# The output projection as two row tiles of TensorE, one step per slice, with a new step order

## The chip, the cores and the metric

The kernel runs on one core of a Trainium2 chip. The metric is the device time of one execution in microseconds (us). Three runs of the kernel before took 1009.82, 1009.85 and 1011.08 us; the median is 1009.85 us. The core has five engines that work in parallel, each in its own written order, and wait for each other by semaphores: TensorE (PE in the rows, its weight loads PEld), VectorE (DVE), ScalarE (ACT), GpSimd (POOL) and SyncE (SP), which issues the DMAs.

## The reference

The input is x (4 x 1024 x 512). A block of windowed attention on 16-channel tokens is followed by a feed-forward block; both are wrapped in layer norms and residual sums. Cut to what matters here:

```python
# tokens of C = 16 channels; q, k, v in two branches of 8 channels, windows of 8 tokens
att = jnp.concatenate([x1, x2], axis=-1) @ proj_w + proj_b      # proj_w is 16 x 16
mu = att.mean(-1, keepdims=True)
var = ((att - mu) ** 2).mean(-1, keepdims=True)
normed = (att - mu) * lax.rsqrt(var + EPS) * ln_w + ln_b
tok = tok + normed
# then: x = x + LN(attn(LN(x)));  x = x + LN(ffn(LN(x)))
# ffn: gate = silu(x @ w_gate * s_gate); up = x @ w_up * s_up; (gate * up) @ w_down * s_down
```

## The kernel before, in words

The 4096 rows are worked on in 8 tiles of 512 rows. The attention of a tile falls into two slices, `p` and `a` of one tile, `b` and `c` of the next. While TensorE computes the feed-forward block of tile t, the other engines and TensorE's gaps compute the attention of tile t+1 and half of t+2. So a tile of the loop holds one feed-forward block and two slices of attention.

A slice runs through steps: `xt` (transposes of x, L581), `qkv` (L589), the products of q and k on VectorE (`qk`, L1093) whose halves GpSimd adds (L924) and VectorE sums (`qk_sum`, L1102), `softmax`, `exp`, the products with v (`pv`, `pv_sum`, the same lines and L933), `attn_out`, then `cat`, `proj`, `square`, `cent_var`, `cent_std`, `cent_out`. `cat` transposes the attention rows of a slice (L600), four of a window's eight rows at a time, and ScalarE copies them into `catt` (L777). `proj` multiplies `catt` by `wproj` (L610). `wproj` is a 128 x 128 matrix that holds the 16 x 16 weights eight times along its diagonal, one block per token of a window, and zeros elsewhere. VectorE adds the bias and writes `cent` (L1159), ScalarE squares it into `csq` (L783), which lies in the memory of `catt`.

`xt`, `qkv`, `cat`, `proj`, `fx` (the transposes of the feed-forward input, L619) and `ln1_fin` (a small matmul for the first norm, L566) share two work banks of PSUM, `ps_w0` and `ps_w1`. A step takes one of them and waits until the step that had it last was read out (`released`, `bank_of`, `bank_free`). In the kernel before `proj` is two steps per slice: `proj 0` (rows 0 to 3 of the windows, bank 0) and `proj 1` (bank 1).

The feed-forward block of a tile runs in 16 groups m. On TensorE a group is `gate` (L629), `up` (L629) and `down` of group m-3 (L649); ScalarE applies silu to gate (L828), VectorE multiplies (`fuse`, L1228), ScalarE and GpSimd split the result in two halves of float16 (`fuse_hi` L834, `fuse_lo` L987). `up` of group m+1 waits for `fuse` of group m, since there is one bank for `up`. 

The order is written out by hand, in tables: `BEFORE` for the part ahead of the first feed-forward block, `STEADY` for tiles 0 to 5 and for the last, `ENDING` for tile 6. In `STEADY` and `ENDING` each step has a slot 3m + i: it stands behind `gate` (i = 0), `up` (i = 1) or `down` and `fuse` (i = 2) of group m, on every engine that takes part in it. SyncE's order comes from the same tables. In the part ahead of the first block ScalarE also casts the 12 parts of the int8 weights to float16 (`cast`, L819); `att_store` of tile 0 (L507: store the attention's rows, then load them as `o1`, L515) waits for all 12 casts, and the load of `xr` (L494) stands behind it in SyncE's queue.

Of the kernel before, what the change touches and what calls it, by code (L numbers as in the profile page):

```python
# [47 lines left out]
Bank = namedtuple("Bank", "ps last")  # L48


def sandwich_kernel(nc, x, qkv_w, conv_w0, conv_b0, conv_w1, conv_b1, proj_w, proj_b, ln_w, ln_b,
                    w_gate, w_up, w_down, s_gate, s_up, s_down, scratch, out):
    with ExitStack() as ctx:
# [245 lines left out]
        START = [("blocks", 0), ("ln1_apply", 0, 0), ("ln1_stats", 0), ("ln1_fin", 0), ("scale_sums", 0),  # L299
                 ("xt", p, 0, 0), ("ln1_apply", 0, 1), ("scale_row", 0), ("token_bias", p), ("xt", p, 0, 1),  # L300
                 ("qkv", p, 0, 0), ("qkv", p, 0, 1), ("scale_pow2", 0), ("qkv", p, 0, 2), ("qkv", p, 0, 3),
                 ("scale_spread", 0), ("qx", p, 0), ("scales", 0)]

        BEFORE = [("qk", p, 0), ("xt", p, 1, 0), ("qk", p, 1), ("xt", p, 1, 1), ("qkv", p, 1, 0), ("qkv", p, 1, 1),
                  ("qk_sum", p, 0), ("qkv", p, 1, 2), ("qk", p, 2), ("qk_sum", p, 1), ("softmax", p, 0),
                  ("qkv", p, 1, 3), ("qx", p, 1), ("qk", p, 3), ("qk_sum", p, 2), ("cast", 0, 0), ("pv", p, 0),
                  ("cast", 0, 1), ("xt", a, 0, 0), ("cast", 0, 2), ("exp", p, 0), ("qkv", a, 0, 0), ("qk_sum", p, 3),
                  ("xt", a, 0, 1), ("token_bias", a), ("pv", p, 1), ("softmax", p, 1), ("pv_sum", p, 0), ("pv", p, 2),
                  ("qkv", a, 0, 1), ("pv_sum", p, 1), ("pv", p, 3), ("xt", a, 1, 0), ("qkv", a, 0, 2), ("warm", 0, 4),
                  ("qkv", a, 0, 3), ("xt", a, 1, 1), ("qk", a, 0), ("pv_sum", p, 2), ("qk", a, 1), ("recip", p),  # L310
                  ("exp", p, 1), ("cast", 0, 3), ("pv_sum", p, 3), ("cast", 0, 4), ("qk_sum", a, 0), ("qkv", a, 1, 0),
                  ("qk", a, 2), ("ln1_stats", 1), ("qx", a, 0), ("qkv", a, 1, 1), ("qk_sum", a, 1), ("qkv", a, 1, 2),
                  ("qkv", a, 1, 3), ("qx", a, 1), ("exp", a, 0), ("ln1_fin", 1), ("attn_out", p), ("ln1_apply", 1, 0),
                  ("softmax", a, 0), ("qk", a, 3), ("cat", p, 0), ("pv", a, 0), ("qk_sum", a, 2), ("qk_sum", a, 3),
                  ("xt", b, 0, 0), ("softmax", a, 1), ("ln1_apply", 1, 1), ("cat", p, 1), ("pv_sum", a, 0),
                  ("proj", p, 0), ("exp", a, 1), ("square", p, 0), ("qkv", b, 0, 0), ("xt", b, 0, 1),
                  ("qkv", b, 0, 1), ("load_xb", 1), ("cast", 0, 5), ("pv", a, 1), ("qkv", b, 0, 2), ("qkv", b, 0, 3),
                  ("pv", a, 2), ("qx", b, 0), ("xt", b, 1, 0), ("pv_sum", a, 1), ("pv", a, 3), ("proj", p, 1),
                  ("pv_sum", a, 2), ("square", p, 1), ("att_store", 0), ("qk", b, 0), ("xt", b, 1, 1), ("cast", 0, 6),
                  ("qkv", b, 1, 0), ("qkv", b, 1, 1), ("pv_sum", a, 3), ("xt", c, 0, 0), ("cast", 0, 7),  # L320
                  ("qkv", b, 1, 2), ("recip", a), ("cent_var", p), ("attn_out", a), ("cent_std", p), ("qkv", b, 1, 3),
                  ("cat", a, 0), ("qx", b, 1), ("cast", 0, 8), ("cent_out", p), ("qk", b, 1), ("qk", b, 2),
                  ("qk_sum", b, 0), ("cat", a, 1), ("proj", a, 0), ("proj", a, 1), ("qk", b, 3), ("qk_sum", b, 1),
                  ("cent_var", a), ("square", a, 0), ("xt", c, 0, 1), ("square", a, 1), ("cast", 0, 9),
                  ("softmax", b, 0), ("qkv", c, 0, 0), ("cent_out", a), ("qkv", c, 0, 1), ("pv", b, 0),
                  ("load_xb", 0), ("token_bias", b), ("qkv", c, 0, 2), ("qk_sum", b, 2), ("qk_sum", b, 3),
                  ("cent_std", a), ("pv", b, 1), ("xt", c, 1, 0), ("warm_cat", a), ("softmax", b, 1), ("exp", b, 0),
                  ("cast", 0, 10), ("pv_sum", b, 0), ("cast", 0, 11), ("qkv", c, 0, 3), ("load_xr", 0),
                  ("qkv", c, 1, 0), ("token_bias", c), ("pv", b, 2), ("pv", b, 3), ("qkv", c, 1, 1), ("pv_sum", b, 1),
                  ("ffn_norm1", 0), ("exp", b, 1), ("xt", c, 1, 1), ("pv_sum", b, 2), ("pv_sum", b, 3),  # L330
                  ("norm1_add", 0), ("qx", c, 0), ("recip", b), ("qkv", c, 1, 2), ("ffn_norm2", 0), ("attn_out", b),
                  ("qkv", c, 1, 3), ("norm2_apply", 0), ("qk", c, 0), ("warm_fx", 0), ("qk", c, 1), ("fx", 0, 0, 0),
                  ("load_xb", 2), ("fx", 0, 0, 1), ("ln1_stats", 2), ("cat", b, 0), ("qk_sum", c, 0)]
# [1046 lines left out]
```

## Time and profile before

| what | value |
|---|---|
| median of three runs | 1009.85 us |
| the profiled execution, its own time | 1010.97 us |
| its span, first to last instruction | 1009.2 us |
| TensorE busy | 906.0 us (90%) |
| VectorE busy | 877.1 us (87%) |
| GpSimd busy | 694.1 us (69%) |
| ScalarE busy | 609.0 us (60%) |
| mean granted clock of TensorE | 0.954 |

The durations of single instructions overlap their successors a little (a product of 2.28 us is followed by the next start 2.20 us later), so sums are best made from start to start. Matmuls of float32 leave two records each, one weight load and one matmul for each of two passes; transposes leave one. The first gate matmul stands at 164.8 us, and the tiles of the loop follow each other every 110.1 us.

### The profile page before, as it was taken

What the parts mean: (1) busy time and instruction counts of PE and PEld (TensorE: products, weight loads), DVE (VectorE), ACT (ScalarE), POOL (GpSimd) and SP (SyncE); (2) the same over time, 40 slices, a digit from 0 to 9 for tenths busy, and PEclk for the clock granted to TensorE, in tenths of its full rate; (3) what the DMA queues carried; (4) which work ended last, traced back from release to release, by engine and by line L of the source; (5) the groups of instructions that cost most, each with busy time, mean ns of one, the idle gap of its engine ahead of it and who ended that gap; (6) DMA issues with size and microseconds to landing.
All of it is one profiled execution on the core that took longest, in us unless ns stands there. A gap on an engine that the chain in (4) does not pass through costs nothing.

```text
span 1009.2 us, 18380 instructions
## 1 busy us (share of the span) xinstructions
PE 906.0 (90%) x6471; PEld 702.4 (70%) x6471; DVE 877.1 (87%) x1309; ACT 609.0 (60%) x1028; POOL 694.1 (69%) x523
## 2 busy tenths in 40 slices
PE   3725627999999999999999999999999999999996
PEld 2514516777777777777777777787778777777773
DVE  4899999999999999999999999999999999553132
ACT  2636634966576855876495657686487665543431
POOL 3556555888679866987778876986788787633323
PEclk9767767999999999999999999999999999999998
DMA  6010070005100510015000510042001300320001
GB/s 178 2 42 0 1 156 11 2 22 128 41 2 1 147 43 21 0 63 124 21 0 5 146 47 10 0 131 56 23 1 60 88 22 1 103 45 22 21 2 42
DMA packets 78318, 46.12 MB, mean 46 GB/s; under 512 B 39608, under 2 KB 72376, under 8 KB 78264
## 3 DMA queue, kind: packets, MB, share of 16 engines
q1 hardware_dynamic: 73400, 45.10, 17.0%
q10 hardware_dynamic: 4864, 0.32, 0.3%
q8 instruction: 32, 0.52, 0.2%
q14 instruction: 22, 0.18, 0.1%
HBM read 28.63 MB, written 16.78 MB: 45 GB/s over the span
## 4 chain that ended last, share of the span: by engine, by line
PE 41%; DVE 22%; POOL 13%; issue 13%; ACT 7%; DMA 2%; POOLq 0%; SPq 0%; DVEq 0%; ACTq 0%
PE ps_gate L629 11%; PE ps_acc L649 11%; PE ps_up L629 11%; DVE prod L1093 7%; POOL sum L933 4%; PE ps_w L589 4%; DVE fuse L1228 2%; POOL cent L458 2%; DVE ps_x L1102 2%; POOL flo L987 2%; DVE attn L1102 1%; PE ps_w L610 1%; DMA xr<-in_L_attn_x 1%; PE ps_w L581 1%; POOL frs L889 1%
## 5 line engine op out<-in xcount | busy, mean ns | idle before, releaser
L1093 DVE TENSOR_TENSOR prod<-ps_x,qkvl 128x2048 f32<-128x2048 f32 x128 | 290.9, 2280 | 2.4 <-POOL sum L933 1.4
L629 PE MATMUL ps_gate<-xhi,wg 128*128 128x256 f16 x1024 | 230.5, 273 | 0.4 <-DVE xlo L1219 0.4
L629 PE MATMUL ps_up<-xhi,wu 128*128 128x256 f16 x1024 | 230.5, 273 | 0.0
L629 PE MATMUL ps_up<-xlo,wu 128*128 128x256 f16 x1024 | 230.5, 273 | 0.0
L629 PE MATMUL ps_gate<-xlo,wg 128*128 128x256 f16 x1024 | 230.5, 273 | 0.0
L987 POOL TENSOR_TENSOR flo<-fuse,fhi 128x512 f16<-128x512 f32 x128 | 148.5, 1161 | 89.1 <-ACT fhi L834 88.3
L828 ACT ACTIVATE gact<-ps_gate,sgate 128x256 f32<-128x256 f32 x256 | 107.2, 470 | 159.4 <-PE ps_gate L629 158.6
L933 POOL TENSOR_TENSOR sum<-prod 128x1024 f32<-128x1024 f32 x64 | 151.4, 2365 | 30.3 <-DVE prod L1093 15.0
L924 POOL TENSOR_TENSOR sum<-prod 128x1024 f32<-128x1024 f32 x64 | 151.1, 2364 | 29.9 <-DVE prod L1093 20.1
L1228 DVE SCALAR_TENSOR_TENSOR fuse<-ps_up,sup,gact 128x256 f32<-128x256 f32 x256 | 110.1, 471 | 69.8 <-PE ps_up L629 61.8
L589 PE MATMUL ps_w<-wqkvl,xt 128*128 128x256 f32 x512 | 137.4, 408 | 21.9 <-ACT xt L747 13.3
L649 PE MATMUL ps_acc<-wd,flo 128*128 128x512 f16 x512 | 153.3, 379 | 0.0
L649 PE MATMUL ps_acc<-wd,fhi 128*128 128x512 f16 x512 | 153.3, 379 | 0.0
L589 PEld LDWEIGHTS ps_w<-wqkvl,xt 128*128 128x128 f32 x512 | 97.3, 204 | 43.3 <-ACT xt L747 18.0
L629 PEld LDWEIGHTS ps_gate<-xlo,wg 128*128 128x128 f16 x1024 | 100.2, 98 | 21.2
L629 PEld LDWEIGHTS ps_gate<-xhi,wg 128*128 128x128 f16 x1024 | 100.7, 98 | 19.8 <-DVE xlo L1219 0.9
L629 PEld LDWEIGHTS ps_up<-xlo,wu 128*128 128x128 f16 x1024 | 100.2, 98 | 13.5
L629 PEld LDWEIGHTS ps_up<-xhi,wu 128*128 128x128 f16 x1024 | 100.2, 98 | 11.4
L756 ACT ACTIVATE qkvl<-ps_w 128x512 f32<-128x512 f32 x128 | 75.4, 598 | 42.4 <-PE ps_w L589 42.2
L649 PEld LDWEIGHTS ps_acc<-wd,flo 128*128 128x128 f16 x512 | 50.1, 98 | 60.4
L834 ACT ACTIVATE fhi<-fuse 128x512 f16<-128x512 f32 x128 | 80.4, 628 | 1.3 <-DVE fuse L1228 1.3
L1102 DVE TENSOR_REDUCE ps_x<-sum 128x256 f32<-128x1024 f32 x64 | 77.6, 1216 | 0.3 <-POOL sum L924 0.3
(148 smaller groups left out, 1383.6 us busy)
## 6 DMA issues: line engine op xcount, KB each, us to landing
xb<-in_L_attn_x SPq DMA_DIRECT2D x64, 128.0 KB, 2.7
attn_rows<-ratt SPq DMA_DIRECT2D x16, 512.0 KB, 3.5
o<-attn_rows SPq DMA_DIRECT2D x32, 256.0 KB, 4.2
xr<-in_L_attn_x SPq DMA_DIRECT2D x16, 512.0 KB
out_x<-y SPq DMA_DIRECT2D x15, 512.0 KB
x<-in_L_ffn_w_gate SPq DMA_DIRECT2D x1, 1024.0 KB, 5.5
xr<-in_L_ffn_w_up SPq DMA_DIRECT2D x1, 1024.0 KB, 8.2
out_x<-y SPq DMA_DIRECT2D x2, 256.0 KB
```

Source lines behind the costliest of these rows:

```text
L589: mm = nc.tensor.matmul(bank.ps[:, 4 * WC * i:4 * WC * i + 4 * WC], xt[:, 2 * wp + i, :], wqkvl[:, br].rearrange("p f x -> p (f x)"), star ...
L629: mm = nc.tensor.matmul(ps[:, HALF * i:HALF * i + HALF], w[:, k, P * j:P * j + P], xs[:, k, rows], start=(k == 0 and part == 0), stop=(k = ...
L649: return nc.tensor.matmul(ps_acc[q][:], f[:, m % SPLITS, HALF * i + P * q:HALF * i + P * q + P], wd[:, 2 * c + i, :], start=(c == 0 and pa ...
L756: nc.scalar.activation(qkvl[:, g, br, :, 2 * wp:2 * wp + 2].rearrange("p f w x -> p w f x"), bank.ps[:].rearrange("p (w f x) -> p w f x", ...
L828: a = nc.scalar.activation(gact[:, m % 2, part], ps_gate[:, part], ACT.Silu, scale=sgate[:, j:j + 1])
L834: nc.scalar.activation(fhi[:, m % SPLITS, :], fuse[:, m % 2, :], ACT.Copy).then_inc(fhi_done, 1)
L924: nc.gpsimd.tensor_tensor(dst.rearrange("p (s c) -> p s c", c=4), s[:, :, 0:4], s[:, :, 4:8], ALU.add).then_inc(half_done, 1)
L933: nc.gpsimd.tensor_tensor(dst.rearrange("p (s j) -> p s j", j=4), s[:, :, 0:4], s[:, :, 4:8], ALU.add).then_inc(half_done, 1)
L987: nc.gpsimd.tensor_tensor(flo[:, m % SPLITS, :], fuse[:, m % 2, :], fhi[:, m % SPLITS, :], ALU.subtract).then_inc(flo_done, 1)
L1093: nc.vector.tensor_tensor(prod[:, half].rearrange("p (s j k) -> p s j k", j=WIN, k=WIN), left[:, :, None, :].broadcast_to([P, 4 * WIN, WIN ...
L1102: nc.vector.tensor_reduce(dst, sum4[:, u % 2, :].rearrange("p (s c) -> p s c", c=4), AX.X, ALU.add).then_inc(sum_done, 1)
L1228: a = nc.vector.scalar_tensor_tensor(fuse[:, m % 2, part], ps_up[:, part], sup[:, j:j + 1], gact[:, m % 2, part], ALU.mult, ALU.mult)
```

## The change: one projection step per slice, on two row tiles

`proj` becomes one step per slice that holds both work banks. Rows 0 to 63 of `catt` (tokens 0 to 3 of each window) are multiplied by the upper left 64 x 64 block of `wproj`, rows 64 to 127 (tokens 4 to 7) by the lower right one. The first result goes to bank 0, the second to bank 1, in turn: 16 matmuls of 64 rows and 64 columns in place of 8 matmuls of 128 rows and 128 columns. VectorE's two additions and ScalarE's two squares stay two, with four tokens of all eight rows each in place of all tokens of four rows. The core of the diff:

```diff
-Bank = namedtuple("Bank", "ps last")
+Bank = namedtuple("Bank", "ps both last")
...
-        def bank_of(step):
-
-            return {"ln1_fin": 0, "fx": step[-1], "xt": step[-1], "qkv": step[-1] % 2, "cat": step[-1],
-                    "proj": step[-1]}[step[0]]
+        def banks_of(step):
+
+            if step[0] == "proj":
+                return 0, 1
+            return (0 if step[0] == "ln1_fin" else step[-1] % 2,)
...
-                        k = bank_of(step)
-                        bank = Bank(ps_w[k], last_use[k])
-                        last_use[k] = (step, tile)
+                        banks = banks_of(step)
+                        bank = Bank(ps_w[banks[0]], ps_w, [(*last_use[k], k) for k in banks if last_use[k]])
+                        for k in banks:
+                            last_use[k] = (step, tile)
...
-            def proj(at, u, bank):
+            def proj(at, bank):
...
-                pe.wait_ge(cat_read, 2 * (2 * at[0] + at[1]) + u + 1)
+                pe.wait_ge(cat_read, 2 * (2 * at[0] + at[1]) + 2)
                 bank_free(bank)
-                for i in range(4):
-                    mm = nc.tensor.matmul(bank.ps[:, P * i:P * i + P], catt[:, u, i, :], wproj[:], start=True, stop=True)
+                for h in range(WIN):
+                    for i in range(2):
+
+                        rows = slice(WC * i, WC * i + WC)
+                        mm = nc.tensor.matmul(bank.both[i][:, WC * h:WC * h + WC], catt[rows, h // 4, h % 4, :],
+                                              wproj[rows, rows], start=True, stop=True)
                 mm.then_inc(proj_done, 1)
...
-                nc.scalar.activation(csq[:, part].rearrange("p h t c -> p (h t c)"),
-                                     cent[:, part].rearrange("p h t c -> p (h t c)"), ACT.Square).then_inc(sq_done, 1)
+                nc.scalar.activation(csq[:, :, part].rearrange("p h t c -> p h (t c)"),
+                                     cent[:, :, part].rearrange("p h t c -> p h (t c)"), ACT.Square).then_inc(sq_done, 1)
...
-                nc.vector.tensor_tensor(cent[:, 4 * u:4 * u + 4].rearrange("p h t c -> p (h t) c"),
-                                        bank.ps[:].rearrange("p (s c) -> p s c", c=C),
-                                        bproj[:, None, :].broadcast_to([P, 4 * WIN, C]), ALU.add).then_inc(proj_read, 1)
+                for i in range(2):
+                    nc.vector.tensor_tensor(cent[:, :, 4 * i:4 * i + 4, :].rearrange("p h t c -> p h (t c)"),
+                                            bank.both[i][:].rearrange("p (s c) -> p s c", c=C),
+                                            bproj[:, None, :].broadcast_to([P, 4 * WIN, C]),
+                                            ALU.add).then_inc(proj_read, 1)
...
-        STEADY = [(0, ("cat", p, 1)), (0, ("proj", p, 0)), (0, ("square", p, 0)), (2, ("qx", a, 1)),
+        STEADY = [(0, ("qk_sum", a, 0)), (0, ("square", p, 0)), (0, ("square", p, 1)), (0, ("proj", p)),
```

All four tables (`START`, `BEFORE`, `STEADY`, `ENDING`) are new. TensorE first, at slice `a` in the middle of a tile. Before (cat, then `proj 0` behind one gate, `proj 1` behind up and down; L600 is cat, L610 proj, L649 down):

```order
L649 MATMUL ps_acc1<-wd,flo 128x512
L600 MATMUL ps_w0<-ident,qkvl 128x128 x4
L600 MATMUL ps_w1<-ident,qkvl 128x128 x4
L629 MATMUL ps_gate<-xhi,wg 128x256
...
L610 MATMUL ps_w0<-wproj,catt 128x128 x4
L629 MATMUL ps_up<-xhi,wu 128x256
...
L649 MATMUL ps_acc1<-wd,flo 128x512
L610 MATMUL ps_w1<-wproj,catt 128x128 x4
L629 MATMUL ps_gate<-xhi,wg 128x256
```

The same place in the changed kernel (L602 is cat, L615 proj, L635 gate and up, L655 down):

```order
L602 MATMUL ps_w0<-ident,qkvl 128x128 x4
L635 MATMUL ps_up<-xhi,wu 128x256
...
L602 MATMUL ps_w1<-ident,qkvl 128x128 x4
L655 MATMUL ps_acc0<-wd,fhi 128x512
...
L655 MATMUL ps_acc1<-wd,flo 128x512
L615 MATMUL ps_w0<-wproj,catt 128x64
L615 MATMUL ps_w1<-wproj,catt 128x64
L615 MATMUL ps_w0<-wproj,catt 128x64
...
L635 MATMUL ps_gate<-xhi,wg 128x256
```

The two cat steps move apart, and 16 small matmuls that change bank at each step follow each other without another instruction between them.

VectorE at the seam between two tiles, that is from `fuse` of group 15 (the first row) to `fuse` of group 0 (the last). Before:

```order
L1228 SCALAR_TENSOR_TENSOR fuse<-ps_up,sup,gact 128x256 x2
L1093 TENSOR_TENSOR prod<-ps_x,qkvl 128x2048
L1102 TENSOR_REDUCE ps_x<-sum 128x256
L1060 BN_STATS bst<-xb 128x6 x8
...
L1054 SCALAR_TENSOR_TENSOR mv<-bst 128x8
L424 UNCONDITIONAL_BRANCH
...
L1159 TENSOR_TENSOR cent<-ps_w,bproj 128x512
...
L1228 SCALAR_TENSOR_TENSOR fuse<-ps_up,sup,gact 128x256 x2
```

In the changed kernel:

```order
L1236 SCALAR_TENSOR_TENSOR fuse<-ps_up,sup,gact 128x256 x2
L1099 TENSOR_TENSOR prod<-ps_x,qkvl 128x2048
L426 UNCONDITIONAL_BRANCH
...
L1108 TENSOR_REDUCE ps_x<-sum 128x256
...
L1166 TENSOR_TENSOR cent<-ps_w,bproj 128x8x64 x2
...
L1236 SCALAR_TENSOR_TENSOR fuse<-ps_up,sup,gact 128x256 x2
L1064 ISA
L1066 BN_STATS bst<-xb 128x6 x8
```

The statistics of the first norm (`BN_STATS`) move from the end of a tile behind the next tile's first `fuse`, the sum (`TENSOR_REDUCE`) across the branch of the loop, and both additions of `proj` now stand together ahead of `fuse` 0.

ScalarE ahead of the first feed-forward block, around the last casts of weights (`wd<-o`, L819 before, L825 in the changed kernel) and the root for the slice `a` of tile 0 (`crs<-cvar`, L808 and L814). Before:

```order
L819 ACTIVATE wd<-o 128x2048
L756 ACTIVATE qkvl<-ps_w 128x2x4x64 x3
L808 ACTIVATE crs<-cvar,epsc 128x64
L747 ACTIVATE xt<-ps_w 128x512
L771 ACT_TABLE_LOAD
L771 ACTIVATE ps_x<-ps_x 128x512
L819 ACTIVATE wd<-o 128x2048 x2
```

In the changed kernel:

```order
L825 ACTIVATE wd<-o 128x2048
L762 ACTIVATE qkvl<-ps_w 128x2x4x64
L753 ACTIVATE xt<-ps_w 128x512
L789 ACTIVATE catt<-cent 128x8x64
L825 ACTIVATE wd<-o 128x2048
L814 ACTIVATE crs<-cvar,epsc 128x64
```

The last two casts now stand ahead of the root, where before they stood behind it.

## Rows read from the trace of the kernel before

**Rows 1.** The page: span and busy time of the engines.
```profile
span 1009.2 us, 18380 instructions
PE 906.0 (90%) x6471; PEld 702.4 (70%) x6471; DVE 877.1 (87%) x1309; ACT 609.0 (60%) x1028; POOL 694.1 (69%) x523
```
**Rows 2.** Busy time by stretch (stretch: length, engines, granted clock, DMA share).
```profile
386.90:497.00 110.10, 108.90 (x804) 84.93 (x803) 107.44 (x157) 74.66 (x129) 87.19 (x63) 1.00 0.18 48
820.00:908.00 88.00, 86.90 (x676) 66.59 (x675) 65.07 (x109) 48.48 (x85) 56.89 (x47) 1.00 0.19 49
```
**Rows 3.** Timeline of DVE in one tile (start, us, line, tile): its idle times.
```profile
521.77 0.88 DVE L1228 SCALAR_TENSOR_TENSOR fuse<-ps_up,sup,gact 128x256 f32<-128x256 f32 x2 [0.37 <-POOL flo L987]
566.78 2.29 DVE L1093 TENSOR_TENSOR prod<-ps_x,qkvl 128x2048 f32<-128x2048 f32 x1 [0.26 <-POOL sum L933]
581.21 2.67 DVE L1210 TENSOR_TENSOR xr<-o,xr 128x512 f32<-128x512 f32 x4 [0.41 <-ACT o L789]
596.97 0.69 DVE L1219 TENSOR_TENSOR xlo<-ps_w,xhi 128x512 f16<-128x512 f32 x1 [0.21 <-ACT xhi L800]
605.89 0.69 DVE L1159 TENSOR_TENSOR cent<-ps_w,bproj 128x512 f32<-128x512 f32 x1 [0.44 <-PE ps_w L610]
```
**Rows 4.** Timeline of PE: a qkv step, and the seam of two tiles.
```profile
515.55 1.03 PE L589 MATMUL ps_w<-wqkvl,xt 128*128 128x256 f32 x4
516.42 0.27 PE L629 MATMUL ps_up<-xhi,wu 128*128 128x256 f16 x1
...
600.03 0.60 PE L600 MATMUL ps_w<-ident,qkvl 128*128 128x128 f32 x4
600.47 1.06 PE L610 MATMUL ps_w<-wproj,catt 128*128 128x128 f32 x8
601.36 0.27 PE L629 MATMUL ps_up<-xhi,wu 128*128 128x256 f16 x1
606.72 0.36 PE L566 MATMUL ps_w<-mv,pair 128*128 128x16 f32 x2 [0.83 <-DVE cent L1159]
606.94 0.27 PE L629 MATMUL ps_gate<-xhi,wg 128*128 128x256 f16 x1
```
**Rows 5.** Timeline of PEld at the start: first loads of 16 and of 128 rows.
```profile
5.32 0.50 PEld L677 LDWEIGHTS ps_acc<-ratt 16*128 16x128 f32 x2 [5.32 <-POOL pair L1021]
13.66 0.50 PEld L566 LDWEIGHTS ps_w<-mv,pair 128*128 128x128 f32 x2 [6.57 <-issue]
```
**Rows 6.** Timeline of DVE, single durations, read from start to start.
```profile
593.88 2.28 DVE L1093 TENSOR_TENSOR prod<-ps_x,qkvl 128x2048 f32<-128x2048 f32 x1
596.08 0.67 DVE L1219 TENSOR_TENSOR xlo<-ps_w,xhi 128x512 f16<-128x512 f32 x1
606.49 0.87 DVE L1228 SCALAR_TENSOR_TENSOR fuse<-ps_up,sup,gact 128x256 f32<-128x256 f32 x2
607.28 1.22 DVE L1102 TENSOR_REDUCE ps_x<-sum 128x256 f32<-128x1024 f32 x1
608.40 0.68 DVE L1159 TENSOR_TENSOR cent<-ps_w,bproj 128x512 f32<-128x512 f32 x1
```
**Rows 7.** The chain of work that ended last (start, us): up and down of TensorE.
```profile
985.50 1.75 PE ps_up L629 x16
987.25 1.73 PE ps_acc L649 x8
```
**Rows 8.** The same chain ahead of the first feed-forward block.
```profile
125.97 3.62 ACT wd L819 x2
130.05 4.70 DMA attn_rows<-ratt
137.41 13.38 DMA xr<-in_L_attn_x
150.81 2.50 DVE xr L1210 x4
```
**Rows 9.** Timeline of DVE ahead of the first feed-forward block.
```profile
125.98 2.11 DVE L466 TENSOR_TENSOR ratt<-cent,xl 128x512 f32<-128x512 f32 x2
```

More of the change, by code:

```diff
@@ L252, in sandwich_kernel, with released @@
         WORK = ("xt", "qkv", "cat", "proj", "fx", "ln1_fin")
-        def released(step, t):
+        def released(step, t, k):
             name, where, *rest = step
@@ L298, in sandwich_kernel @@
         p, a, b, c = (0, 0), (0, 1), (1, 0), (1, 1)
[L299 to L333, printed above, removed]
@@ new lines, in sandwich_kernel @@
+        ENDING = [(0, ("qkv", c, 0, 1)), (0, ("qkv", b, 0, 2)), (0, ("exp", b, 0)), (0, ("qk", a, 2)),
+                  (0, ("load_xr", 1)), (0, ("qk_sum", b, 0)), (0, ("qk_sum", a, 0)), (0, ("ln1_fin", 2)),
+                  (0, ("qkv", b, 0, 3)), (0, ("proj", p)), (1, ("pv", b, 1)), (1, ("qkv", b, 1, 0)),
+                  (1, ("square", p, 0)), (2, ("exp", b, 1)), (2, ("square", p, 1)), (2, ("cent_var", p)),
+                  (3, ("qkv", c, 1, 2)), (4, ("qx", b, 0)), (4, ("xt", b, 0, 1)), (4, ("qk_sum", a, 1)),
+                  (5, ("cent_out", p)), (5, ("qk_sum", b, 1)), (5, ("softmax", a, 0)), (5, ("cent_std", p)),
+                  (6, ("qk_sum", a, 2)), (6, ("qk", a, 3)), (8, ("fx", 0, 1, 0)), (8, ("finish", -1, 1)),
+                  (8, ("exp", a, 0)), (10, ("qx", c, 0)), (11, ("load_xb", 3)), (12, ("pv", a, 0)),
+                  (12, ("qk_sum", a, 3)), (12, ("ln1_apply", 2, 0)), (12, ("pv", a, 1)), (12, ("pv_sum", a, 0)),
+                  (12, ("ln1_stats", 2)), (14, ("softmax", a, 1)), (14, ("fx", 0, 1, 1)), (15, ("cat", b, 0)),
+                  (15, ("finish_apply", -1, 1)), (16, ("finish_add", -1, 1)), (16, ("pv_sum", a, 1)),
+                  (17, ("exp", a, 1)), (17, ("pv", a, 2)), (19, ("pv", a, 3)), (21, ("recip", a)),
+                  (21, ("pv_sum", a, 2)), (22, ("keep_x1", 0)), (22, ("xt", b, 1, 0)), (22, ("pv_sum", a, 3)),
+                  (22, ("attn_out", a)), (22, ("xt", c, 1, 0)), (23, ("att_store", 1)), (24, ("cat", a, 0)),
+                  (24, ("cat", a, 1)), (25, ("square", a, 0)), (25, ("proj", a)), (25, ("qkv", c, 1, 1)),
+                  (25, ("square", a, 1)), (25, ("cent_std", a)), (25, ("softmax", b, 0)), (26, ("qkv", c, 0, 3)),
+                  (26, ("qk", b, 3)), (26, ("cent_var", a)), (26, ("pv", b, 0)), (26, ("recip", b)),
+                  (27, ("cent_out", a)), (27, ("qk", b, 0)), (28, ("qk", b, 2)), (28, ("pv_sum", b, 2)),
+                  (29, ("pv", b, 2)), (31, ("qk_sum", b, 2)), (31, ("token_bias", b)), (32, ("pv_sum", b, 1)),
+                  (32, ("cat", b, 1)), (32, ("token_bias", c)), (32, ("qk_sum", b, 3)), (32, ("qkv", b, 0, 1)),
+                  (33, ("finish", 0, 0)), (34, ("pv", b, 3)), (34, ("qkv", b, 1, 1)), (34, ("attn_out", b)),
+                  (34, ("qkv", c, 0, 2)), (34, ("pv_sum", b, 3)), (34, ("xt", b, 1, 1)), (34, ("qkv", c, 1, 0)),
+                  (36, ("qkv", b, 0, 0)), (36, ("finish_apply", 0, 0)), (36, ("ln1_apply", 2, 1)),
+                  (37, ("xt", c, 0, 1)), (37, ("qkv", c, 1, 3)), (38, ("ffn_norm1", 1)), (39, ("softmax", b, 1)),
+                  (40, ("xt", b, 0, 0)), (40, ("qk", b, 1)), (41, ("qk", c, 0)), (41, ("pv_sum", b, 0)),
+                  (41, ("norm1_add", 1)), (41, ("xt", c, 1, 1)), (41, ("qx", b, 1)), (42, ("qkv", c, 0, 0)),
+                  (42, ("qkv", b, 1, 3)), (42, ("ffn_norm2", 1)), (43, ("xt", c, 0, 0)), (45, ("qx", c, 1)),
+                  (46, ("norm2_apply", 1)), (46, ("fx", 1, 0, 0)), (46, ("fx", 1, 0, 1)), (47, ("qkv", b, 1, 2)),
+                  (47, ("finish_add", 0, 0)), (47, ("qk", c, 1))]
@@ L555, in bank_free @@
             def bank_free(bank):
-                if bank.last:
-                    need(pe, *released(*bank.last))
+                for last in bank.last:
+                    need(pe, *released(*last))
             def ln1_fin(t, bank):
```

125 lines of the change are left out of this document (65 added, 60 removed).

## The prediction

> **What bounds the kernel now.** I read the page's totals first, then the busy time by stretch, then the timelines of VectorE and TensorE in one tile of the loop, and last the chain of waits ahead of the loop. The profiled execution took 1010.97 us, of which 1009.2 are its span [rows 1]; it was 1.1 us above the median of 1009.85. I work out differences from its rows and put them on the median. Below 0.2% (2.0 us) a difference counts as none.
>
> The totals say 90% for TensorE and 87% for VectorE, and both averages mislead. In a tile of the loop, TensorE is busy 108.9 and VectorE 107.4 of 110.1 us [rows 2]. There the two are nearly full together. VectorE's visible idle times in one period are 0.37, 0.26, 0.41, 0.21 and 0.44, together 1.69 us [rows 3], so VectorE has 108.4 us to do per tile. TensorE's work, start to start: 16 gates and 16 ups at 1.75 and 16 downs at 1.73 [rows 7] are 83.7; 16 qkv steps at 0.87 are 13.9; 8 xt, 4 cat and 4 fx steps at 0.44 are 7.0; 4 proj steps at 0.88 are 3.5; `ln1_fin` is 0.22 [rows 4]. Together 108.3. So neither engine can gain much alone: if TensorE became free, VectorE would still need 108.4 of 110.1. Tile 6 is different: there VectorE is busy 65 of 88 us and TensorE 86.9 [rows 2], so from there to the end TensorE's work counts in full.
>
> **The projection on TensorE.** A slice had 8 matmuls, 16 records, in two steps of 0.89 us (600.47 to 601.36) [rows 4], 1.78 in all, or 0.11 per record. Now it has 16 matmuls, 32 records, with half the columns. What sets the pace of a record? The small matmul of `ln1_fin` has 16 columns where proj has 128, and its two records still take 0.22 us (606.72 to 606.94) [rows 4]: 0.11 each. So it isn't the columns that stream but the load of 128 weight columns ahead of each record. Fewer rows don't help either: two loads of 16 rows and two of 128 rows span 0.50 us each [rows 5]. I conclude that each of the 32 records still costs a load of 0.11 us, and the halved columns save nothing. If the two row tiles load side by side, a slice takes 16 x 0.11 = 1.76 us: no gain. If they load one after the other, it takes 32 x 0.11 = 3.52 us, 1.75 more. No row shows two row tiles at work. From below I bound it by the other reading, in which half the columns on two tiles at once make a quarter per matmul: 16 x 2 x 0.11 / 4 = 0.88 us, 0.9 less. I take 1.76, plus up to 0.4 for two seams between whole-array and tiled work, which no row shows either; the step `ln1_fin` to gate, the only similar change of kind, shows no gap (0.22 for two records).
>
> The Trainium skill, "TensorE: Matmul & The Clock Gate", section "LDWEIGHTS (loading the stationary operand)", says that a load takes the number of weight columns divided by 1.2 GHz, whatever the rows: 107 ns. The trace's 0.11 per record agrees. Its page "TensorEngine Tiling (Array Packing)", section "Key Properties", says that different tiles can load and multiply in parallel, and that a change of tiling mode drains TensorE. The first speaks for 1.76, the second against the change; the page gives no price for the drain.
>
> **The other edits.** VectorE's two additions and ScalarE's two squares keep their 512 elements per partition, 0.60 us (605.89 to 606.49) [rows 3, 6] and the like: nothing. They now wait for all 16 matmuls rather than for 8. At the seam VectorE now runs `qk_sum` (1.12) ahead of proj, and TensorE has gate and the step by then; I count nothing. A gain is possible: `ln1_fin` waited 0.83 us for bank 0 in each tile [rows 4]. It now stands two groups of 5.2 us behind proj, so that wait goes. But it was TensorE's wait, and TensorE isn't the only bound, so what is late next is VectorE: at most 0.
>
> **The order in the loop.** VectorE's sum per tile is unchanged, 108.4 us. What changes is how it is spread. `up` of group m+1 waits for `fuse` of group m, so VectorE may lag only a few us. In the new group 5 VectorE has 4 products at 2.20, 3 sums at 1.12, a `fuse` at 0.79 [rows 6] and a row sum of about 0.6, together 13.6 us, while TensorE has a group of 5.23 and two qkv steps, 7.0 [rows 4, 7]. VectorE falls back by 6.6 us in one group. It makes this up only because it runs ahead before. Count the loop that goes along VectorE from `fuse` 2 to `fuse` 12 and along TensorE from `up` 13 to the next tile's `up` 2. On TensorE that piece is 6 ups, 5 gates and 5 downs (27.9), 4 fx and 2 cat steps (2.6), 2 qkv (1.7), proj (1.76) and `ln1_fin` (0.2): 34.2 us. What VectorE does in that time is 4 products (8.8), 4 sums (4.5), 5 fuses (4.0), 6 evictions (3.6) and some 13.3 of statistics and small steps: 34.2 too. So the path is as long as VectorE's own 108.4, with no slack; counted in the same way, the old order had some 0.6. Two more hand-overs between engines, an estimate of 0.1 each from the smallest idle time of 0.21 [rows 3], and unevenness inside the groups put 0 to 0.6 us on a tile, and whatever proj costs above 1.76 adds in full. VectorE's old waits of 1.69 may fall too, since its order was made anew; I take +0.4 per tile, from -0.7 to +1.0. Over 6 tiles: +2.4, from -4 to +6.
>
> **Ahead of the loop.** The chain goes: the last cast ends at 129.6 (125.97 + 3.62), the store of the attention's rows starts at 130.05, `xr` lands at 150.8, and VectorE goes on [rows 8]. VectorE had the rows ready at 128.1 (125.98 + 2.11) [rows 9]. In the new order the last casts stand ahead of the root that precedes these rows, so the store no longer waits for them: -1.5 us. But VectorE has one more sum (1.12) ahead of them, and the load may then meet the same neighbours (13.38 us for 1 MB [rows 8]). I take -1.0, from -4 to +3.
>
> **The last two tiles.** Behind `up` 0 of tile 6 TensorE now has one proj step less (0.88) and one cat step less (0.44), since they stand ahead of it, beside VectorE's work: -1.3 us.
>
> The sum is +2.4 - 1.0 - 1.3 = +0.1, so 1010.0 us. With both seams at 0.4 per slice (13 slices that count) it would be 5 more.
>
> **The rivals.** (1) The loads go in series: the tiles don't run side by side, and the change doesn't do what it says. A proj step costs 3.52. Per tile TensorE has 108.3 + 3.5 = 111.8 us, above VectorE's 108.4; with some 0.8 left of its waits the period is 112.6, 2.5 more. Six tiles give +15, tile 6 with two more steps +3.5 - 1.3, the part ahead of the loop -1 to +2: about +17, 1027 us. It decides from proj at about 2.2 us. For it: both loads of a pair are 128 columns wide, and no row shows two loads at once. Against it: nothing but the page's sentence and that the operands lie in separate rows.
> (2) proj falls to 0.9 to 1.2 us per slice. Then TensorE has 106.6 per tile, VectorE's 108.4 and its waits set the period, and the loop gains 0 to 0.4 per tile (-1). Tile 6 gains two times 0.8, with the -1.3 and -1.0 above: about -5, 1005 us. For it: matmuls half as wide. Against it: [rows 4, 5].
> (3) The loads go side by side, but the crowded group 5 costs VectorE more: GpSimd halves each product and also adds `y` there, and where it is late, as in the 0.26 and 0.37 us of [rows 3], VectorE waits 1.5 us per tile rather than 0.4. That is +9 - 2.3 = +7, 1017 us.
>
> **How the numbers follow.** The forecast with its own range of 1003 to 1014: 0.38. Rival 1: 0.27 (1019 to 1036). Rival 2: 0.20 (1001 to 1008). Rival 3: 0.15 (1014 to 1020). The range reaches into rivals 1 and 2 until some 0.2 are left out: 1002 to 1028. Faster by over 0.2%: rival 2 nearly whole (0.18) and 0.4 of the forecast (0.16), 0.34. Slower: rivals 1 and 3 (0.42) and a small part of the forecast (0.05), 0.47. Within 0.2%: 0.19.
>
> **What would show it.** Forecast: the 32 proj records of a slice take 1.7 to 2.2 us from the first to the next gate, the loads of the two tiles overlap in pairs, the tile period is 109.5 to 111, the wait of `ln1_fin` is gone, and the store starts within 0.7 us of VectorE's last `ratt`. Rival 1: proj takes 3.4 us or more, TensorE's idle time in the loop vanishes and `fuse` waits for `up`. Rival 2: proj near 1 us, period 109.5 to 110. Rival 3: VectorE waits for GpSimd between 30 and 45 us into each tile. I am wrong altogether if the period moves by over 1 us while proj stays at 1.8, or if the part ahead of the loop moves by over 4 us.

## The result and the profile after

The changed kernel took 1037.25 us (median of four runs, 1033.8 to 1038.4) beside 1010.47 for the kernel before on the same chip: 2.5% slower, ratio 1.0251 [1.0230, 1.0272]. The forecast of 1010 with its range to 1028 was wrong.

The page's totals after, which answer to [rows 1]:

```profile
span 1036.3 us, 18846 instructions
PE 919.8 (89%) x6727; PEld 707.3 (68%) x6727; DVE 878.6 (85%) x1309; ACT 607.4 (59%) x1028; POOL 691.1 (67%) x523
```

The span grew by 27.1 us, TensorE's busy time by 13.8, VectorE's by 1.5. Where that lies is told by busy time per stretch, cut at the start of gate 0 of tiles 0, 1, 2, 3, 4, 5 and (last row) from tile 6 to tile 7, the first 0.2 us early; the columns are those of [rows 2]:

```profile
164.10:271.50 107.40, 105.46 (x812) 82.84 (x811) 102.67 (x146) 73.46 (x126) 78.47 (x55) 0.99 0.16 40
271.50:385.50 114.00, 109.65 (x838) 84.75 (x836) 111.31 (x159) 75.91 (x131) 90.47 (x67) 0.99 0.18 48
385.50:503.30 117.80, 113.82 (x834) 87.47 (x834) 107.38 (x156) 74.55 (x128) 86.51 (x64) 0.96 0.18 46
503.30:618.50 115.20, 111.17 (x835) 85.55 (x835) 107.75 (x157) 74.55 (x128) 86.94 (x64) 0.99 0.18 47
618.50:731.90 113.40, 112.44 (x833) 86.89 (x834) 104.35 (x155) 73.17 (x126) 83.54 (x61) 0.97 0.18 47
841.80:936.70 94.90, 91.10 (x732) 68.69 (x731) 69.17 (x113) 51.53 (x89) 61.72 (x51) 1.00 0.18 45
```

The first gate stands nearly where it stood (164.3, before 164.8), and from gate 0 of tile 7 to the end both need 99.6 us. So all of it lies between those gates: 772.4 us for 744.8, 27.6 more. Tiles 1 to 4 take 113.4 to 117.8 for 110.1 [rows 2], and the granted clock is below 1.00 in them. The waits of TensorE in that stretch (engine, tile and line, releaser: us, times, longest) name two that the kernel before has nowhere, for "issue" and for `fuse`:

```profile
PE ps_gate L635 <- issue: 9.4, 3, 3.3
PE ps_up L635 <- DVE fuse L1236: 5.8, 11, 1.6
PE ps_w L625 <- ACT o L801: 1.1, 1, 1.1
PE ps_w L568 <- DVE mv L1060: 1.0, 1, 1.0
```

"Issue" means that TensorE waited for nothing that the profile shows. The timeline of TensorE at gate 0 of tile 2, and the chain of waits from there:

```profile
380.80 1.32 PE L602 MATMUL ps_w<-ident,qkvl 128*128 128x128 f32 x8
385.47 0.39 PE L635 MATMUL ps_gate<-xhi,wg 128*128 128x256 f16 x1 [3.35 <-issue]
385.65 0.42 PE L635 MATMUL ps_gate<-xlo,wg 128*128 128x256 f16 x1
```
```profile
382.12 3.35 issue
385.47 3.59 PE ps_gate L635 x16
389.06 3.61 PE ps_w L615 x32
392.67 2.81 PE ps_up L635 x16
```

The gap stands exactly at the backward branch of the loop over tiles 1 to 4, at all three times that it is taken (3.35, 3.03, 3.05 us), and at none of the seams that are written out (tiles 0, 5, 6). Behind it the gate takes 3.59 us where an `up` of the same size takes 1.75 [rows 7]: the clock is granted at 1.2 GHz in place of 2.4. One more thing is new on the page, the queue of instruction packets. The page after:

```profile
q8 instruction: 61, 1.00, 0.4%
```

On the page of before that queue has 32 packets, 0.52 MB. Around the gap ahead of tile 2 (DMA queues from 382 to 386 us):

```profile
q8 instruction: 2, 0.03, 3.3%
```

The first of the two starts 0.4 us into the gap, the second 0.45 us behind its end. In all nine gaps of this kernel, e2 and e4 (below) gate 0 starts 2.6 to 3.1 us behind the start of such a packet, which itself takes 0.9 to 1.3 us.

### The profile page after: what moved, and what is told of

It is laid out like the page before. It is cut to its first block, busy times and chain, and to the rows that moved or that the text cites. A ratio compares the mean times of both kernels' runs of the same rounds, so it can differ in the third digit from the quotient of the medians.

```text
span 1036.3 us, 18846 instructions
## 1 busy us (share of the span) xinstructions
PE 919.8 (89%) x6727; PEld 707.3 (68%) x6727; DVE 878.6 (85%) x1309; ACT 607.4 (59%) x1028; POOL 691.1 (67%) x523
## 4 chain that ended last, share of the span: by engine, by line
PE 39%; DVE 32%; issue 11%; ACT 9%; POOL 7%; DMA 2%; DVEq 0%; SPq 0%; ACTq 0%; POOLq 0%
PE ps_up L635 10%; DVE prod L1099 9%; PE ps_gate L635 9%; PE ps_acc L655 9%; PE ps_w L591 5%; PE ps_w L615 4%; DVE fuse L1236 3%; DVE ps_x L1108 3%; POOL sum L939 3%; DVE bst L1066 2%; PE ps_w L602 2%; ACT gact L834 2%; DVE attn L1108 1%; DVE y L1258 1%; ACT o L801 1%
## 5 line engine op out<-in xcount | busy, mean ns | idle before, releaser
L635 PE MATMUL ps_gate<-xhi,wg 128*128 128x256 f16 x1024 | 234.3, 275 | 9.8 <-issue 9.4
L635 PE MATMUL ps_up<-xhi,wu 128*128 128x256 f16 x1024 | 232.7, 274 | 5.8 <-DVE fuse L1236 5.8
L635 PE MATMUL ps_gate<-xlo,wg 128*128 128x256 f16 x1024 | 234.4, 275 | 0.0
L635 PE MATMUL ps_up<-xlo,wu 128*128 128x256 f16 x1024 | 232.4, 274 | 0.0
L993 POOL TENSOR_TENSOR flo<-fuse,fhi 128x512 f16<-128x512 f32 x128 | 148.5, 1161 | 99.6 <-ACT fhi L840 99.5
L655 PE MATMUL ps_acc<-wd,fhi 128*128 128x512 f16 x512 | 153.2, 379 | 0.0
L655 PE MATMUL ps_acc<-wd,flo 128*128 128x512 f16 x512 | 153.2, 379 | 0.0
L635 PEld LDWEIGHTS ps_gate<-xhi,wg 128*128 128x128 f16 x1024 | 101.2, 99 | 31.8 <-issue 10.1
L635 PEld LDWEIGHTS ps_gate<-xlo,wg 128*128 128x128 f16 x1024 | 101.1, 99 | 23.4
L635 PEld LDWEIGHTS ps_up<-xhi,wu 128*128 128x128 f16 x1024 | 100.7, 98 | 21.9 <-DVE fuse L1236 9.4
L635 PEld LDWEIGHTS ps_up<-xlo,wu 128*128 128x128 f16 x1024 | 100.7, 98 | 14.4
L655 PEld LDWEIGHTS ps_acc<-wd,flo 128*128 128x128 f16 x512 | 50.1, 98 | 60.4
```

The costliest lines, as they stand in the source:

```text
L635: mm = nc.tensor.matmul(ps[:, HALF * i:HALF * i + HALF], w[:, k, P * j:P * j + P], xs[:, k, rows], start=(k == 0 and part == 0), stop=(k = ...
L655: return nc.tensor.matmul(ps_acc[q][:], f[:, m % SPLITS, HALF * i + P * q:HALF * i + P * q + P], wd[:, 2 * c + i, :], start=(c == 0 and pa ...
L993: nc.gpsimd.tensor_tensor(flo[:, m % SPLITS, :], fuse[:, m % 2, :], fhi[:, m % SPLITS, :], ALU.subtract).then_inc(flo_done, 1)
```

## The experiments

**What the instruction packets say.** Each packet has 16,384 bytes; the programs as built have 64 bytes an instruction, so it carries 256. That fits the program without a loop (e6 below): 54 packets for 13,770 instructions of TensorE in the trace, 255 each on average. The kernel before fetches through the first time of its loop body, then nothing for 346 us (364.3 to 710.5), while the body runs three times more. The changed kernel fetches 8 or 9 packets in every tile of the loop, and 9 from each gap to the next. Its body has 1741 instructions, before 1680: 16 more records a slice, each a load and a matmul, are 64 more instructions a tile, less three waits. Suppose that the program is cut at every 256th instruction, and that the cut lies 180 to 230 instructions behind each multiple of 256. This offset is fitted and was not measured: it is the span that fits all kernels of the table below. Then the body before touches 7 such blocks, the new one 8.

Theory A: TensorE keeps a body of 7 blocks; one of 8 is fetched anew each time (while the last block runs, the one behind it is fetched too), and since the branch's target is gone, TensorE stands until it arrives. Theory B: the gap comes from the new order at the seam.

**Moving the loop.** e1 and e2 put the same 118 idle instructions ahead of the loop of either kernel:

```diff
             pe.wait_ge(setup_pool, SETUP_POOL)
+            for _ in range(236):
+                pe.wait_ge(setup_pool, SETUP_POOL)
```

> The changed kernel with 236 already satisfied waits (118 instructions as built) on TensorE ahead of its first step, so that its loop over tiles 1 to 4 starts 118 instructions later; nothing else. Theory A, instruction store: instruction packets of 16,384 bytes (256 instructions) come at each boundary of 256 in the program; the loop body of 1741 instructions touches 8 such blocks where it stands and 7 when it starts 118 later, as the body of the kernel before (1680) does, which is never fetched again. Then no instruction packet between about 375 and 715 us, the three gaps of 3.0 to 3.4 us ahead of gate 0 are gone, the clock does not fall there, and the time is 1011 to 1021 us. Theory B, the new order: the gaps come from what stands around the seam (the concatenation's second transposes as the last step of the body); the start of the loop doesn't matter, the gaps stay, 1034 to 1041 us. The padding itself costs at most 1 us, in a stretch where TensorE waits for loads.

> The kernel before with the same 118 idle instructions ahead of TensorE's first step; nothing else. Theory A: its body of 1680 instructions then touches 8 blocks of 256 instead of 7, is fetched again in each iteration (8 or 9 packets a tile), and shows gaps of about 3 us ahead of gate 0 at the three taken branches, with a lower granted clock behind each; 1025 to 1036 us. Theory B: the order of the kernel before has no such gap wherever it stands; 1009 to 1012 us.

One thing in both was wrong: the padding cost 14.6 and 13.2 us, since it stood on the chain to the first gate (178.9 and 178.0 us, for 164.3 and 164.8). So e1 took 1030.6 (1.0190 [1.0169, 1.0212]), outside its range, and e2 1033.4 (1.0216 [1.0184, 1.0249]), inside its range only by these 13.2 us. The stretch from the first gate to gate 0 of tile 7 is what tells. (Between e1 and the changed kernel, and between e2 and the kernel before, only the padding differs.)

| kernel | body, instructions | blocks | packets 390 to 722 us | idle by issue | first gate to gate 0 of tile 7 |
|---|---|---|---|---|---|
| before | 2283 to 3962 | 7 | 1 | 0 | 744.8 |
| e2: before, +118 | 2401 to 4080 | 8 | 26 | 7.1 | 755.1 |
| e7: before, +40 | 2323 to 4002 | 7 | 1 | 0 | 744.8 |
| after | 2417 to 4157 | 8 | 25 | 9.4 | 772.4 |
| e1: after, +118 | 2535 to 4275 | 7 | 0 | 0 | 753.2 |
| e3: untiled | 2289 to 3965 | 7 | 1 | 0 | 750.3 |

(The one packet, at 709.2 to 710.5 us, comes 2 us behind gate 0 of tile 5, where the loop is over.) The same move takes the gaps away from one kernel and gives them to the other. A tile of e1, from gate 0 to gate 0:

```profile
396.00:506.50 110.50, 109.50 (x835) 84.62 (x835) 107.65 (x157) 74.52 (x128) 86.85 (x64) 1.00 0.18 47
```

and the waits of TensorE in e2, in the order of before:

```profile
PE ps_gate L629 <- issue: 7.1, 3, 2.6
```

Theory B has fallen. What the gaps cost with what they bring is read from tiles 1 to 4 alone, of the changed kernel and of e1:

```profile
271.50:731.90 460.40, 447.08 (x3338) 344.65 (x3336) 430.79 (x625) 298.18 (x513) 347.46 (x253) 0.98 0.18 47
285.30:727.40 442.10, 438.06 (x3339) 338.73 (x3338) 431.04 (x625) 298.33 (x513) 347.71 (x253) 1.00 0.18 48
```

That is 18.4 of the 27.6 us (from gate to gate 460.5 for 442.1). Another 0.8 lies in tile 0, where the changed kernel has no gap, but its clock was still granted at 1.2 GHz for 1.6 us behind the first gate. In e2 it is 8.7 us in tiles 1 to 4 (448.8 for 440.1), and 1.6 in tile 0 for the same reason.

**Controls.** e5 puts e1's padding where TensorE is idle anyway (96 waits ahead of `("xt", c, 1, 1)` and 140 ahead of `("qkv", c, 1, 2)` in the list BEFORE), e7 a shorter one into the kernel before (80 waits ahead of `("warm_fx", 0)`). e6 has no loop:

```diff
-            with eng.Fori(1, TILES - 3) as t:
-                last_use[:] = [(step, t - 1) for step in last]
+            for t in range(1, TILES - 2):
                 run(MIDDLE, t)
-            last_use[:] = [(step, TILES - 4) for step in last]
-            run(MIDDLE, TILES - 3)
```

> As e1_after_shifted (118 instructions more on TensorE ahead of the loop, so that the body touches 7 blocks of 256 instructions and not 8), but the satisfied waits now stand where TensorE is idle for 7.61 and 10.37 us ahead of the loop, 48 and 70 instructions at 0.12 us each, so that they delay nothing. Theory A: the stretch from the first gate to the last is e1's, 833.9 us against the changed kernel's 853.1, and nothing is added ahead of it: 1016 to 1020 us. If part of e1's gain was an effect of its later first gate, the stretch is longer than 836 us and the time above 1022 us.

> The changed kernel with tiles 1 to 5 written out on every engine, with no loop and no backward branch. TensorE's program is then 13771 instructions, each block of which is fetched once and in order. Theory A: what costs is the fetch at the target of a taken branch, not the number of fetches: 54 or so instruction packets, no gap of issue ahead of any gate, a period of 110.5 us as in e1, 1016 to 1020 us. Rival: it is the fetching as such that disturbs (packets on the same rings as the loads, all through the tile); then the period stays above 112 us and the time above 1025 us.

> The kernel before with 40 idle instructions more (80 satisfied waits) ahead of TensorE's loop, in a stretch where it is idle for 15.76 us. The body then starts 40 instructions later but still touches 7 blocks of 256. Theory A: no gap, no packet during the loop, 1009 to 1012 us. Rival: any shift or any padding of this program brings the gaps (e2's 10.4 us in the loop came from the padding, not from an eighth block): gaps of 2 to 3 us at three seams, 1018 to 1024 us.

e5 took 1019.2 us (1.0074 [1.0057, 1.0091]), 18 less than the changed kernel, with a first gate at 163.7. Its tiles 1 to 4 take 442.0 us, as e1's do; the whole stretch is 2.0 us longer than e1's, all of it in tile 0, where the clock was granted at 1.2 GHz until 168.0 us. e7 took 1011.1 (0.9999 [0.9987, 1.0012]): padding alone does nothing. e6 took 1015.3 (1.0046 [1.0029, 1.0064]), somewhat below its 1016. It fetches more than a body that stays (54 packets on the page, on a queue of their own, q8, where the loads go by q1), and no gate waits for issue. What costs is not to fetch but to branch back to what is gone. Its tiles are even shorter than e1's:

```profile
377.80:487.70 109.90, 109.43 (x837) 84.72 (x836) 107.41 (x157) 74.55 (x129) 86.94 (x64) 1.00 0.18 49
```

The Trainium skill, "Runtime: NRT & Kernel Launch", section "Instruction fetch mechanics", says that TensorE's store holds 2048 instructions in blocks of 256, and that a taken branch whose target isn't in the current window forces a fetch of it before execution can go on. The packets' size and the three gaps agree. So does the count of 9 packets from gap to gap, if one is the block behind the body: 7 blocks and the one behind make 8, which is 2048, and 8 and one don't fit. No run shows the store's size itself. The page also says that the store is two lines with purely sequential prefetch; here the runs differ, since a body of 7 blocks is run three times more without a packet.

**Tiles and order apart.** e3 keeps the new order and the one step, but multiplies as before; e4 only turns the two loops of the step around:

```diff
-                for h in range(WIN):
-                    for i in range(2):
-                        rows = slice(WC * i, WC * i + WC)
-                        mm = nc.tensor.matmul(bank.both[i][:, WC * h:WC * h + WC], catt[rows, h // 4, h % 4, :],
-                                              wproj[rows, rows], start=True, stop=True)
+                for u in range(2):
+                    for i in range(4):
+                        mm = nc.tensor.matmul(bank.both[u][:, P * i:P * i + P], catt[:, u, i, :], wproj[:], start=True, stop=True)
```
```diff
-                for h in range(WIN):
-                    for i in range(2):
+                for i in range(2):
+                    for h in range(WIN):
```

> The changed kernel's order and its one projection step a slice, but the projection as 8 matmuls of 128 rows (16 records) in place of 16 of 64 rows (32 records), four into each bank, with the eviction and the squares laid out as before. The loop body is 64 instructions shorter and touches 7 blocks of 256. Theory A: no gaps at the seams; 1008 to 1017 us, and what is left over 1010 is the new order's. Theory B: the gaps stay, since the order is the same; 1030 to 1038 us.

> The changed kernel with the 16 matmuls of a projection step in another turn: the eight of row tile 0 first, then the eight of row tile 1, so that a record follows one on the same 64 rows. Same number of instructions, so the gaps at the seams stay. If the short step of 1.9 to 2.0 us (0.06 us a record) rests on one row tile being loaded while the other multiplies, a step now takes 2.8 to 3.6 us (0.09 to 0.11 a record, as first loads do), and the time rises by 8 to 24 us over the changed kernel's 1037. If the pace doesn't rest on that, the step stays within 0.2 us of 1.9 to 2.0 and the time within 2 us of it.

e3 took 1014.0 us (1.0034 [1.0023, 1.0044]), e4 1067.3 (1.0582 [1.0536, 1.0628]), more than its 1061; its four runs lie between 1059.6 and 1075.2, and the profile is of the shortest. The projection step and the `up` behind it on TensorE's timeline, of e1, e3 and e4 in this order:

```profile
618.91 2.00 PE L615 MATMUL ps_w<-wproj,catt 64*128 64x64 f32 x32
620.85 0.28 PE L635 MATMUL ps_up<-xhi,wu 128*128 128x256 f16 x1
```
```profile
268.62 1.95 PE L613 MATMUL ps_w<-wproj,catt 128*128 128x128 f32 x16
270.41 0.27 PE L632 MATMUL ps_up<-xhi,wu 128*128 128x256 f16 x1
```
```profile
278.59 3.39 PE L615 MATMUL ps_w<-wproj,catt 64*128 64x64 f32 x32
281.91 0.28 PE L635 MATMUL ps_up<-xhi,wu 128*128 128x256 f16 x1
```

From start to start that is 1.94, 1.79 and 3.32 us. With one tile first and then the other (e4) a record costs 0.10 us, about what one of 128 rows does (1.79 / 16 = 0.11); alternating between the tiles it costs 0.06. So the two tiles do load side by side. The single records of e1's step show it too: the loads start in pairs, 0.007 us apart, and a pair every 0.11 us. This wins back just what twice the number of records costs, less 0.15 us a slice. e1 against e3 gives the price of the tiles without the gaps: 753.22 - 750.25 = 3.0 us, 0.4 in a tile of the loop (110.5 for 110.1). Against before, e3 leaves 5.4 us of that stretch to the new order, 2.7 of them in tile 0 and 2.3 in tile 6, and its first gate comes at 160.8.

**The order's two halves.** e8 is the kernel before with only the lists START and BEFORE of the change, its projection in two steps again and the end joined to the old body:

```diff
-                  ("qk", c, 0), ("qx", c, 1), ("fx", 0, 0, 0), ("fx", 0, 0, 1), ("qk", c, 1), ("cat", b, 0), ("cat", b, 1)]
+                  ("qk", c, 0), ("fx", 0, 0, 0), ("fx", 0, 0, 1), ("qk", c, 1), ("cat", b, 0), ("ln1_stats", 2), ("qk_sum", c, 0)]
```

e9 is e8 with the loop written out as in e6.

> The kernel before, with its untiled projection in two steps, its order inside the tiles, and of the change only the new order ahead of tile 0 (the lists START and BEFORE), joined to the old body by taking the concatenation's second transposes out and putting one sum and the statistics of slice 2 in. In e3 the new head brought the first gate 3.9 us forward (160.8 for 164.8) but tile 0 took 106.1 us for 103.3 and tile 6 94.4 for 92.1. If those losses belong to the new order inside the tiles, they stay away here and the time is 1005 to 1008 us. If the loss in tile 0 is what the earlier first gate left undone (work that the head no longer does), tile 0 stays near 106 us and the time is 1008 to 1011 us.

> e8 (new order ahead of tile 0, old order and untiled projection from there) with tiles 1 to 5 written out, so that TensorE needs no block of its program twice and no register for its waits. Unrolling took the period of the changed kernel from e1's 110.5 us to 109.8 in e6. If that gain is in the loop's bookkeeping, it comes here too, 4 to 5 periods by 0.3 to 0.7 us: 1006 to 1008.5 us. If it belongs to the tiled kernel alone, the time is e8's, 1009 to 1011 us.

e8 took 1009.9 us (0.9983 [0.9974, 0.9993]). Its first gate comes at 161.8, 3.0 earlier, but tile 0 takes 105.2 for 103.3, its loop 110.1 as before and tile 6 92.1 as before. So the new head leaves 1.9 us of its gain for tile 0 to make up, and the order inside the tiles, of which e8 has nothing, holds the rest of e3's loss: 0.9 more in tile 0, and 94.4 for 92.1 in tile 6. In the changed kernel TensorE waits there for `fuse` 1.6 us at once (the 1.6 in the waits above).

e9 took 1006.5 us, inside the 1006 to 1008.5 for a gain that sits in the loop, and the best of all: 0.5% faster than before, 0.9948 [0.9928, 0.9967]. Its stretches from gate 0 to gate 0 of tile 0 and of tile 2:

```profile
161.20:266.30 105.10, 103.42 (x778) 82.29 (x778) 103.25 (x146) 74.28 (x126) 79.39 (x55) 1.00 0.16 41
375.50:484.60 109.10, 108.72 (x805) 84.93 (x804) 107.13 (x157) 74.79 (x128) 87.01 (x64) 1.00 0.19 49
```

Of its 5.0 us against the span before, 3.6 come from the head less 1.8 in tile 0, and the rest from periods of 109.1 to 109.5.

**What an idle stretch costs.** In tiles 1 to 4 of the changed kernel 9.4 us of gaps cost 18.4. Is the other half the clock? e10 and e11 take e6, in which nothing is fetched at a seam, and put 60 and 80 idle instructions ahead of gate 0 of tiles 2, 3 and 4:

```diff
+                if m == 0 and t in (2, 3, 4):
+                    for _ in range(120):
+                        pe.wait_ge(setup_pool, SETUP_POOL)
                 need(pe, silu_done, MB * t + m)
```

> e6 (the changed kernel unrolled: no fetch gap) with 60 satisfied instructions (120 waits, about 7 us of TensorE's queue) ahead of gate 0 of tiles 2, 3 and 4, the places where the changed kernel had its gaps. TensorE's queue runs some 50 instructions ahead of the array there, so that 1 to 4 us of idle time should be left at each. Asked is what an idle stretch without any instruction fetch costs. Theory A2: a gap of about 3 us there costs 6.4 us a seam as in the changed kernel, half of it by the granted clock, which falls behind it; with 3 us of idle the time is 1030 to 1036 us. Rival: the idle time costs itself alone, 3 us a seam, 1022 to 1026 us, and the clock's fall in the changed kernel came with the fetches.

> As e10 with 80 instructions (160 waits) in place of 60, for a second length of the idle stretch: about 2.4 us more of idle time at each of the three places. Theory A2: at least 2.4 us a seam more than e10 and the granted clock at half behind each: 7 to 15 us above e10. Rival: exactly its own 2.4 us a seam, 7 us above e10, with no fall of the clock.

Both lengths missed the aim: the idle time left was 6.05 and about 8.2 us a seam. The 20 instructions between the two runs are worth 2.1 us a seam, 0.11 each, so the 60 of e10 take 6.4 us: TensorE's queue led there by 0.3 us, and not by some 50 instructions. The waits in e10 and in e11:

```profile
PE ps_gate L632 <- issue: 18.2, 3, 6.1
```
```profile
PE ps_gate L632 <- issue: 24.6, 3, 8.2
```

and gate 0 of tile 2 in e10, whose records take 0.42 us where those at 2.4 GHz take 0.27:

```profile
385.52 0.37 PE L632 MATMUL ps_gate<-xhi,wg 128*128 128x256 f16 x1 [6.06 <-issue]
385.69 0.42 PE L632 MATMUL ps_gate<-xlo,wg 128*128 128x256 f16 x1
```

e10 took 1043.5 us (1.0320 [1.0281, 1.0359]), e11 1046.1 (1.0356 [1.0314, 1.0397]). The stretch from the first gate to gate 0 of tile 7 is 777.9 and 780.8, for 750.5 in e6: 18.2 us of idle time cost 27.4, and 24.6 cost 30.3. So idle time without a fetch brings the clock down too; the rival for e10 has fallen. But the price isn't proportional: 6.4 us more of idle time cost 2.9 more, where both theories for e11 said 7 or more. The trace's record of the clock has it at 1.2 GHz for 27.3 us around these seams in e10 and in e11 alike, but in e11 more of that lies inside the idle stretches, where it costs nothing. The 14 us behind gate 0 of tile 3, in e10 and in e11 (the granted clock is 0.57 and 0.87 of full speed):

```profile
503.20:517.20 14.00, 13.98 (x81) 10.02 (x82) 4.52 (x12) 2.59 (x5) 1.40 (x2) 0.57 0.07 25
507.70:521.70 14.00, 14.00 (x113) 10.41 (x114) 7.65 (x25) 3.94 (x8) 1.44 (x3) 0.87 0.01 3
```

Counted from gate 0 on, the clock is low for 18.6 us at the three seams of e10, 11.4 of e11, 19.4 of the changed kernel and 10.2 of e2. Work loses about half of such a time (a gate takes 3.59 us in place of 1.75), and with the idle time this gives the price, in us:

| kernel | idle | half of the low clock behind the gates | sum | measured |
|---|---|---|---|---|
| e10 | 18.2 | 9.3 | 27.5 | 27.4 |
| e11 | 24.6 | 5.7 | 30.3 | 30.3 |
| after | 9.4 | 9.7 | 19.1 | 18.4 |
| e2 | 7.1 | 5.1 | 12.2 | 8.7 |

In e2 the order of before brings waits of TensorE that a late gate swallows: in tiles 1 to 4 they are 4.2 us before and 0.9 in e2, which is 3.3 of the missing 3.5. Why the clock was low for 10.2 us at the gap of 3.35 us and for 3.4 at that of 3.03 stays open.

## Why the prediction was wrong, point by point

- **The projection, 1.76 us a slice.** It measured 1.94, within the 1.7 to 2.2 that was to show it. The working held: a record costs its load, the halved columns save nothing, the two tiles overlap. The 0 to 0.4 for seams between whole-array and tiled work is at most 0.15 a slice (1.94 for 1.79). Rival 1 is what e4 shows: 3.32 us and 20.5 us more than the changed kernel in the stretch. Rival 2 (0.9 to 1.2 us) isn't there.
- **The order in the loop, +0.4 us a tile, +2.4 in all: the step that failed.** As far as it went it was right: 110.5 in e1's loop for 110.1. But it took for granted that TensorE's instructions are always there. The 61 more of them a tile, with the head's 134, moved the body from 7 blocks to 8, so that each taken branch found its target gone; that cost 18.4 us in the loop, about half of it as idle time (9.4) and half by the lower clock behind it. The prediction put this term at nothing without naming it. The prediction's own sign for "wrong altogether" was a period that moves by over 1 us while proj stays at 1.8; that came about. The page of before did show the clue, an instruction queue of 32 packets, where 8375 instructions and three more rounds of 1680 would be 52 blocks, and I didn't ask what made them so few.
- **The same term, tiles 0 and 6.** I gave all six tiles the loop's price. Tile 0 took 3.1 us more (e1 against before), of which e8 puts 1.9 on the new head. The last two tiles were to gain 1.3; tile 6 lost 2.8, tile 5 0.6. I counted TensorE's removed steps and not the wait for `fuse` that the new order put there.
- **Ahead of the loop, -1.0 us.** It measured -0.5, and the store starts 0.02 us behind the last `ratt` (129.29 for 127.17 + 2.10), as said. One profile doesn't fix this size: e11, e10 and e6, which share the head, have their first gate at 162.8, 163.0 and 161.6. Without tiles it comes at 160.8 to 161.9 (e3, e8, e9). In the tiled kernel a projection falls there into a stretch at 1.2 GHz, where a step takes 3.68 us.
- **The wait of `ln1_fin`** for `cent` is gone; one of 1.0 us for `mv` is left (shown above). It brought nothing, as said. Before:

```profile
PE ps_w L566 <- DVE cent L1159: 3.6, 5, 0.9
```

- **Rival 3**, VectorE waiting for GpSimd in the crowded group 5, isn't there. VectorE's waits in the tile of e1 shown above:

```profile
DVE cent L1168 <- PE ps_w L615: 1.0, 2, 0.7
DVE fuse L1238 <- PE ps_up L635: 0.6, 1, 0.6
DVE xlo L1229 <- ACT xhi L808: 0.2, 1, 0.2
```

None is for GpSimd.

The sum after: +18.4 (body in 8 blocks) + 0.8 (clock in tile 0) + 3.0 (tiles) + 5.4 (order) - 0.5 (head) = 27.1, the growth of the span. Of the order's 5.4, 2.7 lie in tile 0 (1.9 with the new head alone) and 2.3 in tile 6. A wait that goes with it was found only in tile 6 (`fuse`); the rest wasn't traced.

## What to carry to other kernels

Before you price the instructions that an edit adds to a loop, count the body's instructions on its engine and where the body starts: here 7 blocks of 256 stayed and 8 did not, and a shift by idle instructions ahead of the loop, or writing the loop out, took 18 (e5) to 22 us (e6) off again. Look at the instruction queue's packets inside the loop in both profiles; if there are none before and some after, compare nothing else until that is mended. And twice as many matmuls of half the size on two tiles of rows gain nothing where the weight load sets the pace.
